# Cross-attention rebuilt in a four-layer block: depth-32 score matmuls, one exponential over all heads, reciprocals applied to the outputs

## The reference, cut to what matters

```
Q, K, V = x @ Wq, ctx @ Wk, ctx @ Wv          # 16 heads of width 16
s = Q @ K.T / 4                               # per head, 256 x 77
layer 0: s = s + attn_bias; padded keys get -1e9
layer 2: s gets a causal mask; Q = x, K = V = ctx
layer 3: a score that is exactly 0 becomes -1e30
out = softmax(s) @ V
x = layernorm(x + out @ Wo + bo)
```

## Time and profile before

| | |
|---|---|
| time of three runs | 1238.49, 1242.33, 1244.52 us (median 1242.33) |
| the profiled execution: time, span | 1244.52 us, 1244.5 us |
| busy PE, DVE, ACT, POOL | 912.5, 592.0, 490.1, 464.0 us (73, 48, 39, 37% of the span) |
| instructions PE, DVE, ACT, POOL | 4471, 1268, 1704, 749 |
| a0, a2, a3 | 137.4, 144.1, 157.8 us |
| moved by DMA | 70.90 MB, mean 57 GB/s |

### The profile page before, as it was taken

One profiled execution on the slowest core, in us unless ns is written; L12 is line 12 of the kernel. 1 busy time (PEld: TensorE's weight loads), 2 busy tenths in 40 slices (PEclk: granted clock), 3 DMA queues, 4 the chain that ended last, 5 costly groups with the idle time before them and its releaser, 6 DMA issues. The chain is left out here.

```text
span 1244.5 us, 19137 instructions
## 1 busy us (share of the span) xinstructions
PE 912.5 (73%) x4471; PEld 622.5 (50%) x4472; DVE 592.0 (48%) x1268; ACT 490.1 (39%) x1704; POOL 464.0 (37%) x749
## 2 busy tenths in 40 slices
PE   5699959673069999713888868997999945888732
PEld 3477647441047777502566624664666623566520
DVE  4688836563212222255778823221112154688737
ACT  2488823221023233101777722221222112999910
POOL 4488835231710000074788701110000063556513
PEclk9899979876579999955889978998999965999955
DMA  9900010000211221232800020001111120000002
GB/s 338 362 2 0 0 46 0 9 1 9 105 60 60 63 63 59 69 92 82 309 0 0 1 102 26 21 21 55 45 48 42 41 64 13 1 1 0 1 0 67
DMA packets 60048, 70.90 MB, mean 57 GB/s; under 512 B 8060, under 2 KB 51812, under 8 KB 60004
## 3 DMA queue, kind: packets, MB, share of 16 engines
q1 hardware_dynamic: 55395, 57.80, 13.9%
q0 software_dynamic: 4608, 12.59, 3.1%
HBM read 45.73 MB, written 24.64 MB: 57 GB/s over the span
## 5 line engine op out<-in xcount | busy, mean ns | idle before, releaser
L1411 PE MATMUL PS<-WE,tmp 128*128 x496 | 186.8, 521 | 0.0
L669 ACT ACTIVATE tmp<-tmp,small 128x77 f32<-128x77 f32 x512 | 176.5, 349 | 22.3 <-DVE small L878 19.9
L567 POOL DMA_INDIRECT tmp<-ys,slot_u x48 | 47.5, 990 | 362.2 <-DMA ys<-tmp 342.8
L1067 DVE TENSOR_TENSOR tmp<-PS,tmp 128x352 f32<-128x352 f32 (+1 forms) x78 | 47.5, 608 | 272.6 <-ACT tmp L773 272.6
L1189 PE MATMUL PS<-ident,XN 128*128 128x128 f32 x256 | 54.2, 348 | 147.5 <-DVE XN L834 145.5
L1251 PE MATMUL PS<-tmp 128*128 128x308 f32 x384 | 126.5, 456 | 8.2 <-DVE small L878 3.0
L462 POOL TENSOR_TENSOR tmp<-tmp,small 128x512 f32<-128x512 f32 x96 | 106.0, 1104 | 63.2 <-DVE small L887 62.8
L773 ACT ACTIVATE tmp<-PS 128x352 f32<-128x352 f32 (+1 forms) x78 | 41.4, 530 | 220.1 <-PE PS L1411 220.1
L1411 PEld LDWEIGHTS PS<-WE,tmp 128*128 128x128 f32 x496 | 92.0, 195 | 60.5 <-issue 36.4
L1189 PEld LDWEIGHTS PS<-ident,XN 128*128 128x128 f32 x256 | 35.7, 174 | 167.6 <-DVE XN L834 100.7
L1431 PE MATMUL PS<-WE,tmp 128*128 (+1 forms) x418 | 101.0, 380 | 2.1 <-DVE tmp L1079 2.1
(11 more groups left out here) (183 smaller groups left out, 1581.2 us busy)
## 6 DMA issues: line engine op xcount, KB each, us to landing
tmp<-xs SPq DMA_DIRECT2D x62, 128.0 KB
ys<-tmp SPq DMA_DIRECT2D x62, 128.0 KB, 1.7
xs<-WE SPq DMA_DIRECT2D x4, 1536.0 KB, 11.2
WE<-in_L_w SPq DMA_DIRECT2D x16, 352.0 KB, 7.5
WE<-in_L_rgT SPq DMA_DIRECT2D x8, 512.0 KB, 9.3
WE<-in_L_ruT SPq DMA_DIRECT2D x8, 512.0 KB, 8.9
WE<-in_L_rdT SPq DMA_DIRECT2D x8, 512.0 KB, 9.6
X<-in_x SPq DMA_DIRECT2D x1, 2048.0 KB, 8.3
```

Of the source, the lines that this page charges most:

```text
L567: pool.indirect_dma_start(YG[:, t % 4, k], None, slots[:, :], bass.IndirectOffsetOnAxis(ap=slot_u[:, k, t:t + 1], axis=0)).then_inc(gather ...
L669: last = act.activation(s, s, ACT.Exp, bias=mx[:, q, h:h + 1], accum_out=sm[:, q, h:h + 1])
L1411: last = pe.matmul(PS[:, 2 * q + k, 0:F], XS[:, q, c], w, start=c == 0, stop=c == G - 1)
```

## The change

The diff rewrites the attention of all four compute engines and its preparation.

- The software pipeline of the attention is gone. Each engine runs 43 slots written out (`SLOTS_IN_ALL`), one unit entering per slot; per-batch work is placed by the functions `out_proj_slot` to `transpose_slot`.
- Scores: four matmuls of depth 32 per unit, each two heads (154 columns) against a compact KBD that holds, for every batch, each pair's keys in its 32 rows. KBD is made once per stage: in the setup by ACT out of the key projection (masked by DVE, L975), for a2 by POOL (`context_keys`), for a3 by ACT. The scores go to one PSUM buffer (banks 0 to 3), freed by `s_taken`.
- POOL subtracts the maximum of all 8 heads (L468), ACT takes one exponential over 616 columns, DVE sums all 8 heads (L913).
- The probabilities are not scaled. POOL spreads the 8 reciprocals to 128 columns (`rsx`, L473), PE transposes them with the probabilities (four transposes, four matmuls of 32 columns, one for rsx), and DVE multiplies the outputs with them, for two units at a time, while it moves them out of PSUM (L924).
- VP and VL are made for all batches at once, by `value_blocks`: 16 matmuls with selecting matrices and 8 masked copies on DVE. It is called at the end of the setup, before e1 and at the start of n6.
- The bias bo is added by POOL (L475), the normalisation is done by ACT with scale and shift (needing two more small POOL operations per batch, `negmean` and `SHIFTS`), and queries are made one batch ahead, into two buffers. In a3 ACT copies the scores, scaled (`scores_scaled`), and DVE combines both in one instruction.
- In the setup DVE waits for the small inputs (`small_loaded`, among them the attention bias) before the first normalisation, for ACT's `keybias`.

The diff, cut to the parts named, indentation reduced:

```diff
-ALONE = dict(a0=HG // 2, a2=HG // 2, a3=HG)
+def out_proj_slot(b):
+    return UNITS * b + 9
+def stats_slot(b):
+    return UNITS * b + 9
+def deviations_slot(b):
+    return UNITS * b + 10
+def normalise_slot(b):
+    return UNITS * b + 11
+def amax_slot(b):
+    return UNITS * b + 12
+def transpose_slot(b):
+    return UNITS * b + 14
+def batch_at(slot_of, s):
+    b, j = divmod(s - slot_of(0), UNITS)
+    return b if j == 0 and 0 <= b < B else None
+SLOTS_IN_ALL = transpose_slot(B - 1) + 1
...
+        rows_b = bass.ds(b * T, T)
+        pool.tensor_copy(MEANS[:, rows_b], mv[:, :, 0])
+        pool.tensor_tensor(negmean[:, :], mv[:, :, 0], minus[:, :], ALU.mult)
...
+    def shift_of_rows(n, b):
+        pool.wait_ge(rstd_ready, n + 1)
+        pool.tensor_tensor(SHIFTS[:, b * T:(b + 1) * T], negmean[:, :], RSTDS[:, b * T:(b + 1) * T],
+                           ALU.mult).then_inc(shift_ready, 1)
...
-                pool.tensor_tensor(PN[:, q, 0:CHUNKS * P].rearrange("p (h k) -> p h k", h=HG), s[:, :, 0:HALF],
-                                   spread(rs[:, q], HALF), ALU.mult)
-                pool.tensor_tensor(PN[:, q, CHUNKS * P:PW].rearrange("p (h k) -> p h k", h=HG), s[:, :, HALF:SK],
-                                   spread(rs[:, q], LEFT), ALU.mult).then_inc(p_ready, 1)
...
+            if s < NU:
+                u, q = u0 + s, s % 2
                 pool.wait_ge(max_ready, u + 1)
+                sc = SC[:, s % 4, 0:KW].rearrange("p (h k) -> p h k", k=SK)
+                pool.tensor_tensor(sc, sc, spread(mx[:, q], SK), ALU.add).then_inc(shifted, 1)
+            if 1 <= s <= NU:
+                u, q = u0 + s - 1, (s - 1) % 2
                 pool.wait_ge(rsum_ready, u + 1)
+                after(pool, pt_psum, u - 1 if s > 2 else 0)
+                pool.tensor_copy(rsx[:, q].rearrange("p (h d) -> p h d", d=DH), spread(rs[:, q], DH)).then_inc(rsx_ready, 1)
+            if j == 2 and b < B and stage != "a3":
+                pool.tensor_tensor(x_of(b), x_of(b), repeat(rows[:, 1], T), ALU.add).then_inc(out_bias, 1)
+            bd = batch_at(deviations_slot, s)
+            if bd is not None:
+                after(pool, shift_ready, n_shift + bd)
+                deviations(norms + bd, bd)
+                shift_of_rows(norms + bd, bd)
...
-                for h in range(alone):
-                    s = SC[:, (j - 3) % 4, h * SK:(h + 1) * SK]
-                    last = act.activation(s, s, ACT.Exp, bias=mx[:, q, h:h + 1], accum_out=sm[:, q, h:h + 1])
-                if alone < HG:
-                    act.wait_ge(shifted, u + 1)
-                    s = SC[:, (j - 3) % 4, alone * SK:]
-                    last = act.activation(s, s, ACT.Exp)
-                last.then_inc(exp_done, 1)
...
+            if s < NU:
+                act.wait_ge(shifted, u0 + s + 1)
+                act.activation(SC[:, s % 4, 0:KW], SC[:, s % 4, 0:KW], ACT.Exp, scale=FAR if stage == "a3" else 1.0).then_inc(exp_done, 1)
+            if 1 <= s <= NU:
+                u = s - 1
+                act.wait_ge(pt_psum, u0 + u + 1)
+                after(act, ot_ready, (u0 + u) // 2 - 1 if u >= 4 else 0)
+                act.activation(PT[:, u % 4], PT_PSUM, ACT.Copy).then_inc(pt_ready, 1)
+            if stage == "a3" and s + 2 < NU:
+                scores_scaled(s + 2)
+            bn = batch_at(normalise_slot, s)
+            if bn is not None:
+                n = norms + bn
+                act.wait_ge(shift_ready, B * layer + bn + 1)
+                after(act, xt_psum, n)
+                if stage == "a3":
+                    after(act, amax_taken, bn)
+                for t in range(T):
+                    row = bn * T + t
+                    last = act.activation(XN[:, t], X[:, row], ACT.Identity, scale=RSTDS[:, row:row + 1],
+                                          bias=SHIFTS[:, row:row + 1])
+                last.then_inc(xn_ready, 1)
...
+    def value_blocks(layer):
+        first = firstmask[:, :].unsqueeze(1).unsqueeze(3).to_broadcast([P, B // 2 * CHUNKS, 2, DH])
+        left = spread(leftmask[:, :], DH).unsqueeze(1).to_broadcast([P, 2 * G, HG, DH])
+        for i in range(B // 2):
+            dve.wait_ge(blocks_psum, 4 * layer + i + 1)
+            dve.tensor_tensor(VP[:, 4 * i:4 * i + 4].rearrange("p n c (i d) -> p (n c) i d", i=2),
+                              PS[:, FIRST_BANK + i % 2].rearrange("p (n i d) -> p n i d", i=2, d=DH), first, ALU.mult)
+            dve.tensor_tensor(VL[:, 4 * i:4 * i + 4].rearrange("p n (h d) -> p n h d", h=HG),
+                              PS[:, LEFT_BANK + i % 2].rearrange("p (n h d) -> p n h d", n=4, h=HG),
+                              left, ALU.mult).then_inc(blocks_ready, 1)
...
+        def biased_scores(k):
+            row = k // UNITS * T + k % T
+            dve.wait_ge(s_psum, u0 + k + 1)
+            after(dve, pt_psum, u0 + k - 3 if k >= 4 else 0)
+            sc = SC[:, k % 4, 0:KW]
+            if stage == "a3":
+                dve.wait_ge(s_copied, k + 1)
+                dve.scalar_tensor_tensor(out=sc, in0=S_PSUM, scalar=0.0, in1=Z[:, k % 2], op0=ALU.is_equal,
+                                         op1=ALU.subtract, reverse1=True).then_inc(s_taken, 1)
+            else:
+                bias = BIAS[:, row].unsqueeze(1).unsqueeze(1).to_broadcast([P, CHUNKS, 2, SK])
+                dve.tensor_tensor(sc.rearrange("p (c h k) -> p c h k", c=CHUNKS, k=SK),
+                                  S_PSUM.rearrange("p c (h k) -> p c h k", k=SK), bias, ALU.add).then_inc(s_taken, 1)
+            dve.drain()
+            after(dve, shifted, u0 + k - 1 if k >= 2 else 0)
+            dve.tensor_reduce(mx[:, k % 2], sc.rearrange("p (h k) -> p h k", h=HG), AX.X,
+                              ALU.max, negate=True).then_inc(max_ready, 1)
+        def reciprocal_sums(k):
+            q = k % 2
+            dve.wait_ge(exp_done, u0 + k + 1)
+            after(dve, pt_psum, u0 + k - 1 if k >= 2 else 0)
+            dve.tensor_reduce(sm[:, q], SC[:, k % 4, 0:KW].rearrange("p (h k) -> p h k", k=SK), AX.X, ALU.add)
+            dve.drain()
+            dve.reciprocal(rs[:, q], sm[:, q]).then_inc(rsum_ready, 1)
+        def scaled_outputs(pair):
+            b, g = divmod(pair, G)
+            dve.wait_ge(pv_done, u0 + 2 * pair + 2)
+            if g == 0 and b >= 2:
+                dve.wait_ge(o_psum, SUM[stage] + b - 1)
+            first = 2 * (pair % 2)
+            dve.tensor_tensor(OT[:, b % 2, g].rearrange("p (t s) -> p t s", t=T),
+                              PS[:, BANK_OT, g * S:(g + 1) * S].rearrange("p (t s) -> p t s", t=T),
+                              PT[:, first:first + 2, (CHUNKS + 1) * P:], ALU.mult).then_inc(ot_ready, 1)
+        dve.memset(SC[:, :, KW:SCW], 0.0)
+        dve.drain()
+        for s in range(SLOTS_IN_ALL):
+            if s < NU:
+                biased_scores(s)
+            if s % 2 == 0 and 4 <= s <= NU + 2:
+                scaled_outputs((s - 4) // 2)
+            if 1 <= s <= NU:
+                reciprocal_sums(s - 1)
+            b = batch_at(stats_slot, s)
+            if b is not None:
+                if stage != "a3":
+                    dve.wait_ge(out_bias, B * layer + b + 1)
+                add_sum(stage, b)
+                row_stats(norms + b, b)
...
+    dve.wait_ge(small_loaded, 16 * 5)
+    dve.drain()
+    for g in range(G):
+        last = dve.tensor_scalar(keybias[:, g], pairmask[:, :], vecs[:, 1, g:g + 1], None, ALU.mult)
+    last.then_inc(vecs_ready, 1)
     dve.wait_ge(x_loaded, 16)
     plain_norm("setup")
-    dve.wait_ge(small_loaded, 16 * 5)
...
     values_evacuate(0, True)
-    dve.memset(PS[96:P, BANK_PT + 1, 0:P], 0.0)
+    value_blocks(0)
     dve.wait_ge(kt_ready, G)
-    dve.tensor_tensor(KT, KT, repeat(MASKF, G), ALU.mult)
-    dve.tensor_scalar(vecs[:, 0], vecs[:, 0], DH ** -0.5, None, ALU.mult)
+    for g in range(G):
+        for h in range(2):
+            k = KBD[:, g, :, h * SK:(h + 1) * SK]
+            last = dve.tensor_tensor(k, k, MASKF.rearrange("p (b k) -> p b k", b=B), ALU.mult)
+    last.then_inc(kbd_ready, 1)
...
+    def value_blocks(layer):
+        for i in range(B // 2):
+            if i >= 2:
+                pe.wait_ge(blocks_ready, 4 * layer + i - 1)
+            for rows_of, bank in ((firstrows, FIRST_BANK), (leftrows, LEFT_BANK)):
+                for c in range(2):
+                    last = pe.matmul(PS[:, bank + i % 2, c * D:(c + 1) * D], rows_of[0:SK, :], V[:, 2 * i + c],
+                                     start=True, stop=True)
+            last.then_inc(blocks_psum, 1)
...
+        def scores(k):
+            b, g, t = k // UNITS, k % UNITS // T, k % T
+            if stage != "a2":
+                pe.wait_ge(q_ready, q0 + b + 1)
+            after(pe, s_taken, u0 + k if k else 0)
+            for c in range(CHUNKS):
+                at = slice(2 * DH * c, 2 * DH * (c + 1))
```

(45 more changed lines are left out.)

384 lines of the change are left out of this document (150 added, 234 removed).

## The result

| | before | after |
|---|---|---|
| median | 1243.4 us (4 runs) | 1365.3 us (4 runs, 1358.3 to 1370.2) |
| ratio | 1 | 1.099, 95% interval 1.094 to 1.104 |
| profiled execution, span | 1244.5 us | 1368.5 us, mean clock 0.80 |

The changed kernel is 10% slower. I had forecast slower, by 4%: 1291 us, at most 1325. The sign was right, the size was wrong by 74 us.

What follows compares the result with a forecast made beforehand. Before, four engines near 90% busy in a0, ACT in a3; after, PE's chain behind POOL's wait. Attention +16.7, setup +21.2, n6 +8.4, small ones +3: +49.3, about 1291 us; own range 1275 to 1305, whole range 1240 to 1325.

Steps and rivals of the forecast that it cites:

- DVE's own work per batch, 13.0 us: Attention: DVE needs 13.0 us per batch if nothing is waited for, 1.7 less than 14.75.
- Waits in each slot at the high level: a0: PE waits for POOL's spread reciprocals before its work; slots of 2.95 to 6.2 make a batch 17.05 against 14.75.
- The wait for the projection: a0, slot j1: DVE's sum with x waits for PE's output projection in the same slot, idling about 1.6 us.
- The failed step: PE's chain in a slot, priced from the kernel before's rows, such as five transposes 0.54 and output projection 1.84.
- POOL's burst: Slot j2: POOL's bias 1.40 and deviations 1.26 precede its subtraction; PE's next transposes start at 1.65 to 1.75, not 0.6.
- Scores, 0.5: PE's scores of a unit in four row groups take 0.5 us, between bounds of 0.35 and 1.03.
- Rival A: PE's row groups don't overlap, scores take 1.03, each late slot 0.45 to 0.5 longer: 1318 us; chance 0.12.
- Transposes, 0.89: PE per unit: four plain transposes, one for rsx and four column pieces, 0.54 + 0.35 = 0.89 us.
- Rival A': PE loses up to 0.17 at each change of its array's split, three more per unit: 1315 us; chance 0.08.
- Setup, +21.2: Setup: DVE's wait for small inputs 8.8, value blocks with last copies 11.1, key masks 1.3, sum +21.2 us.
- n6, +8.4: Start of n6: the same value blocks, warm, 7.4, with PE's first transposes behind them, 1: +8.4 us.
- Rival B: Attention waits are hidden, DVE runs at its own 13.0 us per batch in all stages: 1227 us, faster; chance 0.15.

Runs made afterwards that it cites:

- run with later statistics: The combined kernel's preparation; in the attention PE issues next scores ahead of queries and output projection, DVE's sum with x and statistics one slot later: 1243.2 us, ratio 1.002.
- with fillers: Changed kernel plus constant transposes on PE, 8 and 12 at two places of a batch, where it waits for the spread reciprocals: 1323.0 us, ratio 1.068.
- The combined kernel: Changed kernel with reciprocals' wait last, POOL's jobs moved, queries behind values, DVE's scaling behind its sum, preparation reordered, n6's block copies one batch later: 1229.7 us, ratio 0.990.

## Why the prediction was wrong, point by point

- **DVE's own work per batch, 13.0 us.** Right: 13.0 was reached in a2 of the run with later statistics.
- **Waits in each slot at the high level.** Right in mechanism and, in a0, nearly in size. The forecast's batch was 2.95 + 2.95 + 4.95 + 6.2 = 17.05; with fillers and a clock of 1.00 it is 2.88 + 2.88 + 5.35 + 6.20 = 17.31. The wait for the projection, forecast 1.6, is 1.73.
- **The failed step: "Before's rows give: five transposes 0.54", and so on, used for every slot.** All PE durations were taken from rows at 2.4 GHz, in a kernel whose PE was busy 13.58 of 14.75 us. The change puts PE idle, 0.6 us in each slot by my own count and 1.91 in one by the trace, and I never asked what the clock would do. For a2 I wrote that I keep the clock "as it is"; it fell from 0.88 to 0.69. The fillers give back 47.8 us of the three stages, two thirds of the 72 that the forecast missed (88.9 less 16.7). The remaining 24 us lie in a0 (160.8 with fillers against 153.9 forecast), a2 (156.7 against 146.1) and a3 (163.1 against 156). In a2 and in a0 part of it is clock again: with fillers it is still 0.86 and 0.92, and the 2.83 us at 703.47 stand behind PE at the low level. In a3 it is a wait: slot j0 takes 6.94 us (1207.79 to 1214.73) at a clock of 1.00 where I had 4.8, and 1.38 of it is PE standing before the queries until ACT has copied XT, a wait that the forecast does not have. How the 24 us divide between the two was not separated by a run.
- **POOL's burst.** Forecast as a cost to the slot after, 1.1 us later. Its place was right for a2, where it is PE's wait of 1.89 in j0; moving it gave 17.6 us there, more than a wait of 1.1 in eight batches, and the clock rose from 0.82 to 0.92. In a0 the queries, which stand ahead of the same transposes, cover it.
- **Scores, 0.5.** Right: the row groups overlap. Eight records stand in 0.54, and from their start to PE's next instruction it is 0.48 (in the batch with fillers, 146.88 to 147.36), less than half of 1.03. Rival A, 1.03, is out. The Trainium skill, "TensorE: Matmul & The Clock Gate", Part 3, has 3.07x for four row groups; by these two numbers it is 1.03 / 0.48 = 2.1 for 154 columns.
- **Transposes, 0.89.** Too small: from the first to the values' start it is 145.56 - 144.45 = 1.11 with fillers. Four plain transposes take 0.59 where 0.54 was for five, which is 0.16 more than four fifths of that; behind the queries, with no row-group scores ahead, they take 0.53 (153.90 to 154.43), which leaves 0.10 before the column pieces. The transpose of rsx, 0.17, is 0.06 above its share. Rival A' had that mechanism; at 0.2 per unit it is 19 us for 96 units if all were on the path, and the batch at 17.31 shows that little of it is. The Trainium skill, "TensorEngine Tiling (Array Packing)", Key Properties, says that a change of the tiling mode drains TensorE; the trace agrees so far as time is lost at these changes, 0.10 to 0.16 us in four transposes, but does not show the drain itself.
- **Setup, +21.2.** Measured +25.7. The norm chain moved from 9.17 to 18.63, 9.5 where 8.8 were forecast. The blocks were sized at 9.7 from the earlier trace rows, a stage where the clock came back; they ran at the low level throughout, 14.0 us, which is nearly the whole miss of 4.5.
- **n6, +8.4.** The stages r2 to n6 grew by 10.1; the 1.7 above the forecast stay open.
- **Rival B**, DVE bound and faster, did not happen, but its condition was named: waits fitting under DVE's own time. The combined kernel comes there in a2.

## What to carry to other kernels

A wait added ahead of all of PE's work can cost twice, as here: once as a wait, and again through the clock. Price each PE duration at both levels whenever a change makes PE stand where it did not before, and read the granted clock of the stretch next to the time. When spare waits are left, the cheap test is filler matmuls inside them; the cure is to put the wait only in front of the instruction that needs it, and per-batch jobs where their engine stands idle anyway.

## What the runs showed of the hardware that I had not expected

PE fell to half its rate inside a batch, after 1.91 us of waiting that followed another 0.35, and came back in the same batch: the four transposes that took 1.11 us at 134.67 take 0.60 at 141.67. The batches around it (109 to 189 us) do the same, though the moment of the fall moves by up to 1 us, so a mean clock of 0.83 is two levels in turn. The length of the last wait alone does not tell it: the wait of 1.40 us before the transposes at 90.18 leaves them at 0.66, that before those at 96.67 is as long, and they take 1.01. And twenty needless matmuls per batch, 2.6 us of busy time, made it 2.8 us shorter.
